# Row sums of two heads by accumulating DMAs instead of GpSimd additions and ones matmuls

## The reference

```
scores = einsum('bhqd,bhkd->bhqk', q, k) / sqrt(32)
attn = softmax(scores, axis=-1)
out = einsum('bhqk,bhkd->bhqd', attn, v)
```

## Time and profile before

| | us |
|---|---|
| median of 3 runs | 3496.42 |
| lowest and highest run | 3493.79, 3498.39 |
| the profiled execution, its time | 3486.67 |
| its span, first to last instruction | 3485.4 |

### The profile page before, as it was taken

The page is one execution under the profiler, slowest core; times in us unless marked ns, Lnnn a source line. Parts: engine busy times, 40 slices in busy tenths (PEclk is TensorE's granted clock), DMA queues, the critical chain, the costliest instruction groups (busy, mean ns, idle before and its releaser), DMA issues.

```text
span 3485.4 us, 49344 instructions
## 1 busy us (share of the span) xinstructions
PE 3383.5 (97%) x18874; PEld 2226.1 (64%) x18874; DVE 2153.9 (62%) x3650; ACT 1446.7 (42%) x2803; POOL 1780.9 (51%) x836
## 2 busy tenths in 40 slices
PE   8789999999999999999999998899999999999999
PEld 7677655555555555555555552678888888778888
DVE  4548677777777777777777778643333333226666
ACT  2111366666666666666666656221111111112322
POOL 0200499898888989888898977320000000002222
PEclk9899999999999999999999999999999999999999
DMA  5363400303003030030210000841111110311221
GB/s 199 137 205 129 132 19 11 80 13 77 19 10 80 10 67 23 19 79 11 43 46 19 22 13 1 283 158 37 37 37 37 37 37 14 108 46 61 70 72 57
DMA packets 140498, 222.77 MB, mean 64 GB/s; under 512 B 14148, under 2 KB 56380, under 8 KB 137191
## 3 DMA queue, kind: packets, MB, share of 16 engines
q1 hardware_dynamic: 140263, 219.62, 21.5%
HBM read 143.55 MB, written 75.50 MB: 63 GB/s over the span
## 4 chain that ended last, share of the span: by engine, by line
PE 92%; DVE 4%; DMA 1%; issue 1%; POOL 1%; ACT 1%; SPq 0%; DVEq 0%; ACTq 0%; POOLq 0%
PE ps L337 17%; PE ps L632 14%; PE ps L620 13%; PE ps L1120 10%; PE ps L1109 10%; PE ps L639 4%; PE ps L432 4%; PE ps L1640 3%; PE ps L1653 2%; PE ps L436 2%; PE ps L982 2%; DVE pacc L802 2%; PE ps L1673 2%; PE ps L1470 1%; PE ps L151 1%; PE ps L1664 1%
## 5 line engine op out<-in xcount | busy, mean ns | idle before, releaser
L362 DVE TENSOR_REDUCE nmp<-ps 128x1 f32<-128x512 f32 x2048 | 1287.2, 683 | 411.8 <-PE ps L337 411.2
L726 ACT ACTIVATE pt<-ps 128x512 f32<-128x512 f32 x2048 | 1064.7, 603 | 638.3 <-PE ps L620 622.1
L821 POOL TENSOR_TENSOR pacc<-pacc,pt 128x1024 f32<-128x1024 f32 x420 | 1000.4, 2382 | 119.1 <-ACT pt L726 93.0
L337 PE MATMUL ps<-ks,qs 96*128 96x512 f32 x2048 | 871.5, 426 | 18.5 <-DVE nmp L362 17.1
L620 PE MATMUL ps<-qs,ks 128*128 128x512 f32 x2048 | 818.0, 404 | 16.6 <-ACT pt L726 13.0
L337 PEld LDWEIGHTS ps<-ks,qs 96*128 96x128 f32 x2048 | 387.3, 189 | 446.7 <-DVE nmp L362 256.9
L632 PE MATMUL ps<-pt,vq 128*32 128x512 f32 x4096 | 547.3, 606 | 0.2 <-ACT pt L726 0.2
L620 PEld LDWEIGHTS ps<-qs,ks 128*128 128x128 f32 x2048 | 388.6, 191 | 110.0 <-ACT pt L726 43.6
L829 POOL TENSOR_TENSOR paccb<-paccb,pt 128x1024 f32<-128x1024 f32 x172 | 424.8, 2470 | 10.9 <-ACT pt L726 8.5
L1109 PE MATMUL ps<-hpb,w 128*128 128x512 f32 x1536 | 382.0, 398 | 3.4 <-DMA x_d<-x 3.4
L1120 PE MATMUL ps<-w,gp 128*128 128x512 f32 x1536 | 380.1, 396 | 2.6 <-DVE gp L1253 2.6
(11 more groups left out here) (172 smaller groups left out, 3232.4 us busy)
## 6 DMA issues: line engine op xcount, KB each, us to landing
qk_d<-st SPq DMA_DIRECT2D x128, 256.0 KB, 2.7
ks<-qk_d SPq DMA_DIRECT2D x24, 1024.0 KB, 12.5
qs<-qk_d SPq DMA_DIRECT2D x96, 256.0 KB, 5.3
xina<-in_x SPq DMA_DIRECT2D x8, 1024.0 KB, 6.3
v_d<-vst SPq DMA_DIRECT2D x32, 256.0 KB, 2.4
vq<-v_d SPq DMA_DIRECT2D x8, 1024.0 KB, 17.9
ao_d<-aop SPq DMA_DIRECT2D x8, 1024.0 KB, 5.3
ao<-ao_d SPq DMA_DIRECT2D x32, 256.0 KB, 4.5
```

Of the source, the lines that this page charges most:

```text
L337: pe.matmul(ps[:, cnt.bank["max", u], :], qsb[0:96, v % 4, hh, 128 * qt:128 * qt + 128], ksb[w % 2][0:96, hh, CH * kc:CH * kc + CH], start ...
L362: dve.tensor_reduce(nmp[:, hq, kc:kc + 1], ps[:, cnt.bank["max", u], :], AX.X, ALU.max, negate=True).then_inc(s_mr, 1)
L726: act.activation(pt[:, g % 4, half, c0:c0 + CH], ps[:, (n + 1) % 3, :], ACT.Exp, scale=SCALE).then_inc(s_exp, 1)
L821: pool.tensor_tensor(pacc[:, v % 2, :], pt[:, (g - 1) % 4, 0, :] if kt == 1 else pacc[:, v % 2, :], pt[:, g % 4, 0, :], ALU.add).then_inc( ...
```

## The change

- `pool_kts`, `paccb`, `pe_sums` and bank 5's sums go. For every group POOL issues a DMA of pt's half 1 (128 rows of 4 KB) into `half[v % 2][kt % 3]`: a plain copy at kt 0, 1 and 2, an accumulating one (it adds to what is there) from kt 3 on. Before it issues one it waits until the one into the same buffer, three groups before, has landed.
- TensorE sums the three buffers over the partitions at kt 4 of the next chunk (three sets, accumulated in the left half of a bank), and then pacc (one set, the right half), instead of at kt 1. The transposes move from kt 3 and 5 to kt 6 and 9.
- ACT may write half 1 of a slot when the DMA of four groups before has landed. It copies all sums at once; `accs` and `accv` have one buffer instead of two.
- The queries have three slots instead of four: at kt 0 of chunk v (from 1 on) SP asks for chunk v + 2. `wtmpo` lies where K's first buffer is.
- In chunks 30 and 31 DVE still adds pacc, and POOL only issues DMAs.

```diff
-def pool_kts(v):
-    return tuple(range(1, 14)) if v >= NU - 2 else (2, 3, 5, 6, 9, 11, 12)
+NA = 3
+
+def half_count(v, kt):
+    a = kt % NA
+    return 16 * ((v // 2) * ((15 - a) // NA + 1) + kt // NA + 1)
...
-        qsb = take("qs", [128, 4, 4, CH], F32R)
+        qsb = take("qs", [128, 3, 4, CH], F32R)
...
-        paccb = take("paccb", [128, 2 * CH])
-        accv = take("accv", [128, 2, CH])
-        accs = take("accs", [128, 2, CH])
+        half = take("half", [128, 2, NA, 2 * CH])
+        accv = take("accv", [128, CH])
+        accs = take("accs", [128, CH])
...
-        def pe_sums(g):
-            v, kt = divmod(g, 16)
-            if kt not in pool_kts(v):
-                if kt == 0 and v:
-                    pe.wait_ge(s_accs, v)
-                pe_ones(5, pt[:, g % 4, 1, :], kt == 0, kt == 15, s_ones)
-            if kt == 14:
-                pe.wait_ge(s_add, cnt.addb[16 * v + pool_kts(v)[-1]])
-                pe_ones(5, paccb[:, :], False, False, s_ones)
...
         def pe_sums_end(v):
+            pe_bank_free(("sums", v))
+            for a in range(NA):
+                pe.wait_ge(s_half[v % 2][a], half_count(v, (15 - a) // NA * NA + a))
+                pe_ones(cnt.bank["sums", v], 0, half[:, v % 2, a, :], a == 0, a == NA - 1)
...
-            pe_ones(cnt.bank["sums", v], pacc[:, v % 2, :], True, True, s_last)
+            pe_ones(cnt.bank["sums", v], 256, pacc[:, v % 2, :], True, True).then_inc(s_last, 1)
...
-                if kt == 1 and v:
+                if kt == 4 and v:
                     pe_sums_end(v - 1)
...
-                elif e in cnt.ones:
-                    act.wait_ge(s_ones, cnt.ones[e])
                 else:
-                    act.wait_ge(s_add, cnt.addb[max(e, 16 * ev + pool_kts(ev)[1])])
+                    act.wait_ge(s_half[ev % 2][ekt % NA], half_count(ev, ekt))
...
-                if kt in kts[1:]:
-                    pool.wait_ge(s_exp, 4 * g + 4)
-                    if kt > kts[1]:
-                        pool.wait_ge(s_add, cnt.addb[16 * v + kts[kts.index(kt) - 1]])
-                    elif v:
-                        pool.wait_ge(s_ones, cnt.onesb[v - 1])
-                    pool.tensor_tensor(paccb[:, :], pt[:, (g - 1) % 4, 1, :] if kt == kts[1] else paccb[:, :],
-                                       pt[:, g % 4, 1, :], ALU.add).then_inc(s_add, 1)
+                pool.wait_ge(s_exp, 4 * g + 4)
+                to = half[:, v % 2, kt % NA, :]
+                if kt >= NA:
+                    pool.wait_ge(s_half[v % 2][kt % NA], half_count(v, kt - NA))
+                    pool.dma_start(to, pt[:, g % 4, 1, :], accum_op=ALU.add).then_inc(s_half[v % 2][kt % NA], 16)
+                else:
+                    if v >= 2:
+                        pool.wait_ge(s_last, v - 1)
+                    pool.dma_start(to, pt[:, g % 4, 1, :]).then_inc(s_half[v % 2][kt % NA], 16)
...
-                if kt == 0 and v + 3 < NU:
-                    if v >= 1:
-                        sp.wait_ge(s_sc, 64 * v)
-                    sp_load_q(v + 3)
+                if kt == 0 and v >= 1 and v + 2 < NU:
+                    sp.wait_ge(s_sc, 64 * v)
+                    sp_load_q(v + 2)
```

More of the change, by code:

```diff
@@ L35 @@
 STEPS = 66
-def pool_kts(v):
-    return tuple(range(1, 14)) if v >= NU - 2 else (2, 3, 5, 6, 9, 11, 12)
+NA = 3
+def half_count(v, kt):
+    a = kt % NA
+    return 16 * ((v // 2) * ((15 - a) // NA + 1) + kt // NA + 1)
 class Counts:
     def __init__(self):
-        self.add, self.addb, self.late, self.ones, self.onesb = {}, {}, {}, {}, {}
-        pa = pd = po = 0
+        self.add, self.late = {}, {}
+        pa = pd = 0
         for g in range(NGRP):
             v, kt = divmod(g, 16)
-            if kt not in pool_kts(v):
-                po += 1
-                self.ones[g] = po
-            if kt == 14:
[L56 to L65, removed]
+            if kt and v >= NU - 2:
+                pd += 1
+                self.late[g] = pd
+            elif kt:
                 pa += 1
-                self.addb[g] = pa
+                self.add[g] = pa
         self.bank, self.before = {}, {}
@@ L78, in __init__ @@
             for hh in range(4):
-                if kt == 3 and hh == 1 and v:
+                if kt == 6 and hh == 1 and v:
                     self.use(("turn_sums", v - 1))
-                elif kt == 5 and hh == 1 and v:
+                elif kt == 9 and hh == 1 and v:
                     self.use(("turn_values", v - 1))
@@ L261, in program @@
         rs = take("rs", [128, 16])
-        wtmpo = take("wtmpo", [128, NK, D])
+        wtmpo = place("wtmpo", [128, NK, D], (base + 31) // 32 * 32)
         wo = place("wo", [128, 2, NK, D], nc.sbuf_top - 16384, F32R)
+        s_half = [[sem(f"s_half{i}{j}") for j in range(NA)] for i in range(2)]
         s_vq = [sem(f"s_vq{i}") for i in range(2)]
         s_ao = [sem(f"s_ao{i}") for i in range(2)]
-        (s_sc, s_exp, s_pv, s_ones, s_add, s_late, s_accv, s_accs, s_last, s_lasts, s_at, s_rec, s_an, s_on, s_wo) = (
-            sem(n) for n in ("s_sc", "s_exp", "s_pv", "s_ones", "s_add", "s_late", "s_accv", "s_accs", "s_last",
+        (s_sc, s_exp, s_pv, s_add, s_late, s_accv, s_last, s_lasts, s_at, s_rec, s_an, s_on, s_wo) = (
+            sem(n) for n in ("s_sc", "s_exp", "s_pv", "s_add", "s_late", "s_accv", "s_last",
                              "s_lasts", "s_at", "s_rec", "s_an", "s_on", "s_wo"))
@@ L333, in pe_max @@
             if n == 0:
-                pe.wait_ge(s_qd[v % 4], 48 * (v // 4 + 1))
+                pe.wait_ge(s_qd[v % 3], 48 * (v // 3 + 1))
                 pe.wait_ge(s_kd[w % 2], 48 * (w // 2 + 1))
             pe_bank_free(("max", u))
-            pe.matmul(ps[:, cnt.bank["max", u], :], qsb[0:96, v % 4, hh, 128 * qt:128 * qt + 128],
+            pe.matmul(ps[:, cnt.bank["max", u], :], qsb[0:96, v % 3, hh, 128 * qt:128 * qt + 128],
                       ksb[w % 2][0:96, hh, CH * kc:CH * kc + CH], start=True, stop=True).then_inc(s_mm, 1)
@@ L634, in pe_values, with pe_ones @@
             m.then_inc(s_pv, 1)
-        def pe_ones(bank, src, start, stop, done):
+        def pe_ones(bank, c, src, start, stop):
             for r in range(4):
                 c0 = CH * (r // 2) + 256 * (r % 2)
-                m = pe.matmul(ps[32 * r:32 * r + 32, bank, 0:256], ones[:, :], src[:, c0:c0 + 256],
-                              start=start, stop=stop)
-            m.then_inc(done, 1)
-        def pe_sums(g):
-            v, kt = divmod(g, 16)
-            if kt not in pool_kts(v):
-                if kt == 0 and v:
-                    pe.wait_ge(s_accs, v)
-                pe_ones(5, pt[:, g % 4, 1, :], kt == 0, kt == 15, s_ones)
-            if kt == 14:
-                pe.wait_ge(s_add, cnt.addb[16 * v + pool_kts(v)[-1]])
-                pe_ones(5, paccb[:, :], False, False, s_ones)
+                m = pe.matmul(ps[32 * r:32 * r + 32, bank, c:c + 256], ones[:, :], src[:, c0:c0 + 256],
+                              start=start, stop=stop, skip_group_check=True)
+            return m
         def pe_sums_end(v):
+            pe_bank_free(("sums", v))
+            for a in range(NA):
+                pe.wait_ge(s_half[v % 2][a], half_count(v, (15 - a) // NA * NA + a))
+                pe_ones(cnt.bank["sums", v], 0, half[:, v % 2, a, :], a == 0, a == NA - 1)
             if v >= NU - 2:
@@ L699, in pe_attention @@
                     step += 1
-                pe_sums(g)
-                if kt == 1 and v:
+                if kt == 4 and v:
                     pe_sums_end(v - 1)
@@ L729, in act_sums_end @@
             act.wait_ge(s_last, v + 1)
-            act.activation(accs[:, v % 2, 256:512], ps[:, cnt.bank["sums", v], 0:256], ACT.Copy).then_inc(s_lasts, 1)
+            if v:
+                act.wait_ge(s_at, 2 * v - 1)
+            act.activation(accs[:, :], ps[:, cnt.bank["sums", v], :], ACT.Copy).then_inc(s_lasts, 1)
         def act_attention():
@@ L745, in act_attention @@
                     act.wait_ge(s_pv, g + 1)
[L746 to L751, removed]
+                    if v:
+                        act.wait_ge(s_at, 2 * v)
+                    act.activation(accv[:, :], ps[:, 4, :], ACT.Copy).then_inc(s_accv, 1)
+                if kt == 4 and v:
                     act_sums_end(v - 1)
@@ L866, in sp_attention @@
                 for hh in range(4):
-                    if kt == 3 and hh == 1 and v:
+                    if kt == 6 and hh == 1 and v:
                         continue
-                    if kt == 5 and hh == 1 and v:
+                    if kt == 9 and hh == 1 and v:
                         if v % NCH == 0:
@@ L910, in attention_over @@
             eng.wait_ge(s_lasts, NU)
-            eng.wait_ge(s_add, max(cnt.addb.values()))
+            eng.wait_ge(s_last, NU)
             eng.wait_ge(s_wlo, 16)
@@ L1051, in program @@
             "s_f1", "s_g", "s_gh", "s_gl", "s_f2", "s_rb", "s_ro"))
-        s_rd, n_rd = s_qd, 3 * NU // 4
```

(1 more changed line is left out.)

19 lines of the change are left out of this document (8 added, 11 removed).

## The result

| | us |
|---|---|
| before, median of 4 runs | 3497.40 |
| after, median of 4 runs | 3527.35 (3522.35 to 3528.06) |
| ratio | 1.0085, interval 1.0063 to 1.0107 |
| the profiled execution, its time and span | 3528.06, 3526.7 |

A forecast was written before the change was run, and what follows sets the result against it. TensorE was taken to bound the kernel, POOL second and near. Terms -91 - 1 - 6 + 63 + 4 = -31 on the profiled 3486.7 us gave 3455.7, or 3465 as median; own range 3425 to 3490, wider range 3405 to 3650.

The forecast's parts named there:

- The price of the ones matmuls: In chunks up to v = 29, TensorE drops from 11 ones sets to 4, at 0.44 us each: -91 us.
- DVE's additions: In chunks 30 and 31, DVE's additions take 1.2 us instead of 3.2: -7 and +1, net -6 us.
- POOL's issues: POOL's 16 DMA issues per chunk take about 1.0 us each, just hidden while under 1.05 us.
- POOL is the bound: Rival, chance 0.22: POOL issues above 1.25 us each make POOL the limit; at 1.6 us, 3658 us.
- D: What one accumulating DMA into half costs the 16 engines: taken as 2.4 us, hidden up to 2.95.
- double read: Rival, chance 0.17: both passes of an accumulating DMA cost in full, 3.2 us, chunk as long as before: 3515 us.
- The landing: A 512 KB DMA into half lands in about 4 us, or 5 to 6 with a second read.
- The wait for queries: At v = 4, 8, ..., 24, TensorE waits 10.5 us each for queries requested behind K and V: +63 us.
- ACT for the one four groups back, about 12 us: both are covered in a quiet chunk: ACT's wait for the DMA into half four groups earlier, and POOL's for three, are covered in a quiet chunk.
- 4 us to v = 0: Chunk 0, where K and V are loaded too and accumulations are late, waits another 4 us.
- my -31: The forecast's sum for the whole kernel: -91 - 1 - 6 + 63 + 4 = -31 us.
- The q wait at its full price: Rival, chance 0.09: six waits for queries of 19 us each, 114 us, more than the 98 saved: 3516 us.

The follow-up runs named there:

- plain: The changed kernel with plain copies for all 16 DMAs of a chunk, no accumulation, row sums of heads 2 and 3 taken from pacc: 3501.28 us, ratio 1.0016.
- v_moved: The changed kernel with V's load moved from between K and the queries to the next chunk: 3456.44 us, ratio 0.9882.
- q_first: The changed kernel with SP asking for the queries of chunk v + 2 ahead of K and V: 3461.97 us, ratio 0.9905.
- spread: The changed kernel with queries first, K in 12 pieces of 256 KB and V in four, issued singly over four chunks: 3404.37 us, ratio 0.9739.
- pieces_at_once: The spread kernel with K's 12 pieces issued together at the start of each four chunks: 3445.93 us, ratio 0.9839 to the kernel before.

## Why the prediction was wrong

**The price of the ones matmuls**: right. 3.1 us a chunk forecast, about 3.15 measured in 23 quiet chunks, which last 52.5 us against 52.6: 95 us in 30 chunks. (7 x 0.44 x 30 is 92, not 91.)

**DVE's additions**: 1.2 us each, as forecast; the row for the kernel after says min/median/max 1160/1225/1227 ns. Chunk 30 gained 10 us (7 forecast). The end of the stage lost 2.6 us (1 forecast): TensorE stands 5.6 us until the last accumulation has landed, and its last matmuls run at the lower clock (a granted clock of 0.50 from 2199 to 2204 us).

**POOL's issues**: 0.99 us for an accumulating DMA (1.0 taken, limit 1.05), 0.58 for a copy. POOL is busy 48.1 of 52.4 us. The rival "POOL is the bound" did not come true. The recorded 0.99 is more than an issue takes away from the additions, as the next addition's row starts before the issue's row ends:

```profile
934.86 0.88 POOL L810 DMA_DIRECT2D half<-pt  x1
935.59 2.55 POOL L804 TENSOR_TENSOR pacc<-pacc,pt 128x1024 f32<-128x1024 f32 x1
937.91 1.06 POOL L810 DMA_DIRECT2D half<-pt  x1
```

One issue and one addition take 937.91 - 934.86 = 3.05 us, as long as a group of TensorE's (3.06).

**D**: 2.82 us, not 2.4, and under the limit of 2.95. The 2.4 was near by luck, from two errors that nearly cancel. I took one and a half passes, with reads and writes partly overlapping; it was two full ones, as in the rival "double read". And a pass was 1.39 us instead of the 1.6 that I had from the earlier trace rows. The rule of the Trainium skill (Collectives: The Full Stack, on ReduceScatter and AllGather) is that a reduce needs two source reads where a copy needs one. The trace agrees with it: 2.82 us against 1.39. The landing was sized near: 5.0 us for an accumulating DMA (5 to 6 forecast), 2.9 in `plain` for a copy (about 4 forecast).

**The wait for queries**: 10.5 us forecast for each, 54.4 / 6 = 9.1 measured, a right size for a reason half right. I had divided the engines' time by bytes. `plain` halves the time that the DMAs into half take of the engines and the wait stays; `v_moved` takes V away and the wait is gone. What holds the queries is that SP's issue of the first one, behind V, lasts 18.8 us. Whether V's short rows (512 bytes) or its place make it last so long is not shown: no run changed the rows.

**The step that failed** is "ACT for the one four groups back, about 12 us: both are covered in a quiet chunk". I priced that wait for quiet chunks, and then gave the loading ones only the wait for queries, and 4 us to v = 0. There a DMA into half lands up to 19 us after its issue (18.5 in chunk 8), ACT may not write the slot, and TensorE stands 4.5 to 6.8 us more, in chunk 0 even 10.9. `q_first` shows it alone: no wait for queries, and 7 to 13 us of excess left. `spread` against `pieces_at_once` puts it on K in one lump. Behind each of the two holes comes slow work at the lower clock, about 2 to 3 us a hole, that the sum did not have either. With 19.8 us in place of 10.5, six times, and 13 in place of 4, my -31 becomes +34. Less 3 for chunk 30 and 4 for the ones matmuls, plus 2 for the end, it is +29, what the chunks add up to.

The two nearest rivals came near the 3527 by luck. "The q wait at its full price" gave 3516 from one wait of 19 us; there were two, of 9.1 and 5.4 us on average, and slow work behind them. "Double read" gave 3515; its two full passes are what D shows, but D stayed under its 3.2, the quiet chunks kept their gain, and `plain`, without the second read, keeps 17 us of the 20.

That K's own long packets (rows of 8 KB onto 32 partitions) are what makes the other queue slow is not shown: no run changed their shape at a fixed place. That lumps of K are, was shown by `spread` against `pieces_at_once`. The packet records of the traces add that pacing makes K itself cheaper: its 8 KB packets take a median of 564 ns in the changed kernel and 545 in `pieces_at_once`, but 412 in `spread`.

## What to carry to other kernels

Moving work from a busy engine to idle DMA engines makes every transfer that was free before a rival of it: price the new transfers not in the quiet stretch but in the one where the old ones come in lumps, and look for each wait whose cover is counted in groups. Then pace the old loads in small pieces, each just in time, and let no load with an early deadline stand behind one that holds the issuing engine, as the queries stood behind V. Here the change was worth -2.6% with that, +0.9% without, and pacing without the change nothing.

## What the runs showed of the hardware

- A 512 KB accumulating DMA within SBUF takes the 16 engines 2.8 us, a copy 1.4. POOL's issue is recorded with 0.99 us and 0.58. Issue to landing is 5.0 us (median of the accumulating ones) against 2.9 (copies in `plain`); the copies that go among accumulating DMAs take 5.9.
- The DMA engines stood 97% busy in a stretch of `spread` with paced loads, and TensorE did not wait. A lump of 3 MB, with the same bytes in four chunks, delayed DMAs of another queue from 5 us to 18.5 (19.9 in `v_moved`, where V is not in the lump); with pacing the longest took 13.2.
- The three query loads behind K and V keep SP for 13.8 us without DMAs from POOL and for 20.2 with them, behind K alone for about 3.
- POOL's additions are not slowed by the accumulating issues between them. Their recorded length grows from 2.37 to 2.49 us, but from an addition's start to the next issue's it is 2.33 us in both (median of some 450 in `after` and in `plain`).
- A hole of 7 or 8 us in TensorE's work is followed by tiles 0.42 us apart instead of 0.23 for about 5 us, at a granted clock of 0.50.
